# A new order of steps on every engine of a Mamba-2 layer with a ternary feed-forward part

## What is computed

```python
# mixing part, then layer norm
zxbcdt = u @ W_in.T                       # 512 -> 2184: z 1024, x 1024, B 64, C 64, dt 8
dt  = softplus(zxbcdt[..., -8:] + dt_bias)
xBC = silu(causal_conv_4_taps(xBC) + conv_b)
y   = ssd(x, dt, -exp(A_log), B, C) + x * D     # 8 heads of 128, state 64
yg  = y * silu(z)
yn  = yg * rsqrt(mean(yg * yg) + 1e-5) * norm_w
x1  = layernorm(u + yn @ W_out.T)
# feed-forward part, then layer norm
wu, wg, wd = ternary(W_up), ternary(W_gate), ternary(W_down)   # -1, 0, 1 times mean(|W|)
out = layernorm(x1 + (silu(x1 @ wu.T) * (x1 @ wg.T)) @ wd.T)   # 2048 inner features
```

## Time and profile before

| | |
|---|---|
| median of the runs | 1609.8 us |
| the profiled execution, own time | 1608.34 us |
| its span in the trace | 1606.6 us |
| TensorE busy | 1533.0 us, 95% |
| VectorE, ScalarE, GpSimd busy | 59%, 44%, 24% |
| granted TensorE clock, mean | 0.98 |
| HBM traffic | 57 GB/s over the span |

### The profile page before, as it was taken

How to read it: one execution, slowest core, us unless ns; L and a number is a source line. 1 busy time by engine, 2 the same in 40 slices (tenths; PEclk the granted TensorE clock), 3 DMA queues, 4 the chain that set the end, 5 groups by cost and what they waited for, 6 DMA issues and landing times.

```text
span 1606.6 us, 23426 instructions
## 1 busy us (share of the span) xinstructions
PE 1533.0 (95%) x9012; PEld 1300.0 (81%) x9012; DVE 953.7 (59%) x2026; ACT 710.0 (44%) x1364; POOL 391.7 (24%) x504
## 2 busy tenths in 40 slices
...
GB/s 237 66 21 86 86 73 16 85 86 73 39 62 86 86 57 31 86 86 70 18 89 305 71 7 53 1 17 36 7 47 0 53 0 29 25 14 40 0 27 27
DMA packets 38687, 92.38 MB, mean 58 GB/s; under 512 B 4144, under 2 KB 4656, under 8 KB 38576
## 3 DMA queue, kind: packets, MB, share of 16 engines
...
...
## 4 chain that ended last, share of the span: by engine, by line
PE 66%; DVE 18%; ACT 7%; issue 4%; POOL 4%; DMA 1%; SPq 0%; DVEq 0%; POOLq 0%; ACTq 0%
PE ps L366 30%; PE ps L387 14%; PE ps L221 10%; DVE s_mm L771 7%; PE ps L310 6%; DVE s_xact L692 3%; POOL s_mm L997 2%; ACT s_mm L525 2%; PE ps L264 2%; PE ps L281 2%; DVE s_ygr L798 1%; ACT L532 1%; DVE s_bcacc L692 1%; DVE s_sc L731 1%; ACT s_xT L514 1%
## 5 line engine op out<-in xcount | busy, mean ns | idle before, releaser
L366 PE MATMUL ps<-s_x1h,s_tern 128*128 128x512 f32 x1024 | 406.9, 397 | 3.2 <-DVE s_x1l L871 3.2
L366 PE MATMUL ps<-s_x1l,s_tern 128*128 128x512 f32 x1024 | 405.2, 396 | 0.0
L221 PE MATMUL ps<-s_uhi,s_whi 128*128 128x256 f32 x1088 | 323.1, 297 | 20.0 <-DVE s_xact L692 13.8
L221 PE MATMUL ps<-s_ulo,s_whi 128*128 128x256 f32 x1088 | 313.0, 288 | 0.0
L221 PE MATMUL ps<-s_uhi,s_wlo 128*128 128x256 f32 x1088 | 312.5, 287 | 0.0
L881 DVE TENSOR_TENSOR s_hf<-s_sil,ps 128x512 f32<-128x512 f32 x128 | 87.9, 687 | 330.1 <-PE ps L366 330.0
L221 PEld LDWEIGHTS ps<-s_uhi,s_whi 128*128 128x128 f32 x1088 | 211.9, 195 | 56.2 <-DVE s_xact L692 31.1
L366 PEld LDWEIGHTS ps<-s_x1h,s_tern 128*128 128x128 f32 x1024 | 193.3, 189 | 49.5 <-DVE s_tern L865 3.6
L366 PEld LDWEIGHTS ps<-s_x1l,s_tern 128*128 128x128 f32 x1024 | 193.4, 189 | 45.1
L221 PEld LDWEIGHTS ps<-s_ulo,s_whi 128*128 128x128 f32 x1088 | 212.0, 195 | 0.0
L221 PEld LDWEIGHTS ps<-s_uhi,s_wlo 128*128 128x128 f32 x1088 | 211.6, 195 | 0.0
...
## 6 DMA issues: line engine op xcount, KB each, us to landing
...
```

What stands on the lines that cost most here:

```text
L221: o = e.matmul(IPB[r % 3][:, 256 * i:256 * i + 256], wt[:, j, kk, :], u[:, kk, :], start=(m == 0), stop=(m == 11))
L366: o = e.matmul(bank[:], tern[:, j, 512 * mi + 128 * k:512 * mi + 128 * k + 128], x[g % 2][:, k, :], start=(m == 0), stop=(m == 7))
```

## The change

The step functions, their waits and all buffers stay as they are. What changes is the order of the calls: in the written-out first two groups, in the loop body of the slots, and in the written-out change to the feed-forward part, on all five engines. The loops of the feed-forward part stay. No step is added or removed. The diff, with the loop body whole and the rest cut:

```diff
@@ TensorE
-        warm()
-        DT(0); ip(0, 0); dtT(0); ip(0, 1); ip(0, 2); ip(0, 3); CUM(0); ip(0, 4); G(0)
-        ip(0, 5); ip(0, 6); ip(0, 7); ip(0, 8)
-
-        DT(1); dtT(1); TR(0, 0); TR(0, 1); ip(1, 0); ip(1, 1); TR(1, 1); TR(1, 0); CUM(1); ip(1, 2); ip(1, 3)
-        ip(1, 4); Y(0); G(1); ST(0); ip(1, 5); Y(1); OP(0); ip(1, 6); SQ(0); ST(1); ip(1, 7); SQ(1)
-        TR(2, 1); TR(2, 0); ip(1, 8); TR(3, 0); TR(3, 1)
+        warm(); ip(0, 0); DT(0); ip(0, 1); dtT(0); ip(0, 2); ip(0, 3); CUM(0); ip(0, 4); G(0); ip(0, 5); ip(0, 6)
+        DT(1); ip(0, 7); ip(0, 8); dtT(1); TR(0, 0); TR(0, 1); ip(1, 0); ip(1, 1); TR(1, 1); CUM(1); TR(1, 0)
+        ip(1, 2); ip(1, 3); G(1); Y(0); ip(1, 4); ST(0); ip(1, 5); Y(1); OP(0); SQ(0); ip(1, 6); ip(1, 7); ip(1, 8)
+        TR(2, 1); TR(2, 0); ST(1); SQ(1); TR(3, 0); TR(3, 1)
         for n in range(2, NG):
             c = 2 * n - 2
-            DT(n); OP(c - 1); dtT(n); ip(n, 0); ip(n, 1); ip(n, 2); Y(c); CUM(n); ip(n, 3); ip(n, 4); G(n)
-            ST(c); ip(n, 5); OP(c); Y(c + 1); ip(n, 6); SQ(c); ST(c + 1); ip(n, 7); SQ(c + 1)
-            TR(c + 2, 1); TR(c + 2, 0); ip(n, 8); TR(c + 3, 0); TR(c + 3, 1)
+            DT(n); OP(c - 1); dtT(n); ip(n, 0); ip(n, 1); ip(n, 2); Y(c); CUM(n); ip(n, 3); ST(c); G(n); ip(n, 4)
+            ip(n, 5); OP(c); Y(c + 1); SQ(c); ip(n, 6); ip(n, 7); TR(c + 2, 1); TR(c + 2, 0); ip(n, 8); ST(c + 1)
+            TR(c + 3, 0); SQ(c + 1); TR(c + 3, 1)
         c = NCH - 2
-        OP(c - 1); Y(c); ST(c); T1(0, 1); WT(); T1(0, 0); Y(c + 1); SQ(c); T1(0, 2); T1(0, 3); OP(c)
+        OP(c - 1); Y(c); ST(c); WT(); T1(0, 1); T1(0, 0); T1(0, 2); Y(c + 1); SQ(c); T1(0, 3); OP(c); expert(0, 0, 0)
...
@@ ScalarE
         for n in range(2, NG):
             c = 2 * n - 2
-            f_zs(n - 1, 3); f_xTe(c + 1, 1); f_uhi(n); f_E(c); f_E(c + 1); f_xe(n, 0); f_spexp(n); f_dec(c)
-            f_xTe(c + 1, 0); f_dec(c + 1); f_xe(n, 1)
+            f_uhi(n); f_E(c); f_dec(c); f_zs(n - 1, 3); f_xe(n, 0); f_xTe(c + 1, 1); f_dec(c + 1); f_spexp(n)
+            f_xe(n, 1); f_xTe(c + 1, 0); f_xe(n, 2); f_E(c + 1)
             if n == 2:
-                wabs(4); wabs(5)
-            wabs(3 * n); f_silc(n, 0); f_xe(n, 2); f_silc(n, 1); f_sq(c); f_ygh(c); f_xe(n, 3); f_silc(n, 2)
-            wabs(3 * n + 1); f_xe(n, 4); f_seg(c + 2); f_silc(n, 3); f_silc(n, 4); f_sq(c + 1); wabs(3 * n + 2)
-            f_ygh(c + 1); f_zs(n, 0); f_zs(n, 1); f_zs(n, 2)
+                wabs(4)
+            f_silc(n, 0); f_xe(n, 3); f_sq(c)
+            if n == 2:
+                wabs(5)
+            f_ygh(c); wabs(3 * n); f_silc(n, 1); wabs(3 * n + 1); f_xe(n, 4); f_seg(c + 2); f_silc(n, 2); f_silc(n, 3)
+            f_silc(n, 4); wabs(3 * n + 2); f_sq(c + 1); f_zs(n, 0); f_ygh(c + 1); f_zs(n, 1); f_zs(n, 2)
             if n == NG - 1:
-                f_dec(c + 2); f_E(c + 2)
-            f_xTe(c + 2, 0); f_xTe(c + 2, 1); f_seg(c + 3)
+                f_E(c + 2)
+            f_xTe(c + 2, 0); f_xTe(c + 2, 1)
+            if n == NG - 1:
+                f_dec(c + 2)
+            f_seg(c + 3)
...
@@ VectorE
         for n in range(2, NG):
             c = 2 * n - 2
-            f_ms(c - 1); f_dte(n); f_ulo(n); f_M(c); f_dtr(n); f_r1(c - 1); f_dA(n); f_wz(c); f_wz(c + 1)
-            f_taps(n, 0); f_taps(n, 1); f_M(c + 1); f_gate(c, 0); f_gate(c, 1); f_cte(n); f_taps(n, 2); f_sqsum(c)
-            f_GM(n); f_S(c); f_taps(n, 3); f_taps(n, 4); f_dd(c + 2); f_x1(c - 1); f_gate(c + 1, 0); f_gate(c + 1, 1)
+            f_ms(c - 1); f_ulo(n); f_dte(n); f_M(c); f_dtr(n); f_wz(c); f_taps(n, 0); f_dA(n); f_wz(c + 1)
+            f_taps(n, 1); f_gate(c, 0); f_cte(n); f_taps(n, 2); f_S(c); f_gate(c, 1); f_r1(c - 1); f_M(c + 1)
+            f_sqsum(c); f_GM(n); f_taps(n, 3); f_taps(n, 4); f_ms(c); f_gate(c + 1, 0); f_gate(c + 1, 1); f_dd(c + 2)
+            f_r1(c)
             if n < NG - 1:
                 f_dd(c + 3)
-            f_ms(c); f_sqsum(c + 1)
+            f_sqsum(c + 1); f_x1(c - 1); f_x1(c)
             if n == NG - 1:
                 f_M(c + 2); f_wz(c + 2); wtot()
-            f_r1(c); f_S(c + 1); f_x1(c)
+            f_S(c + 1)
...
@@ GpSimd
         for n in range(2, NG):
             c = 2 * n - 2
-            f_Cexp(c); f_DI(c); f_rs(c - 1); f_edge(n, 0); f_xw(c); f_xw(c + 1); f_edge(n, 1); f_rs1(c - 1); f_Sd(c)
-            f_DI(c + 1); f_Cexp(c + 1); f_edge(n, 2); f_ygl(c); f_edge(n, 3); f_edge(n, 4); f_rs(c)
+            f_DI(c); f_Cexp(c); f_edge(n, 0); f_xw(c); f_Sd(c); f_rs(c - 1); f_xw(c + 1); f_edge(n, 1); f_edge(n, 2)
+            f_ygl(c); f_rs1(c - 1); f_Cexp(c + 1); f_DI(c + 1); f_Sd(c + 1); f_edge(n, 3); f_edge(n, 4); f_rs(c)
+            f_rs1(c)
...
@@ SyncE
         for n in range(2, NG):
             c = 2 * n - 2
-            load_bc(c + 2)
+            load_bc(c + 2); load_r0(c); load_wst(3 * n + 1)
             if n < NG - 1:
                 load_u(n + 1)
-            load_wst(3 * n + 1); load_bc(c + 3); load_wst(3 * n + 2); load_r0(c); load_r0(c + 1); load_wst(3 * n + 3)
-            store_x1(c - 1)
+            load_bc(c + 3); load_wst(3 * n + 2); store_x1(c - 1); load_r0(c + 1); store_x1(c)
             if n < NG - 1:
                 store_ct(n + 1)
-            store_x1(c)
-
+            load_wst(3 * n + 3)
...
```

More of the change, by code:

```diff
@@ L429, in program_pe @@
+        expert(0, 11, 1); down(0, 8); T1(1, 3); down(0, 9)
         for g in range(8):
@@ L610, in program_act @@
-        f_seg(0); f_silc(0, 2); f_zs(0, 1); f_silc(0, 3); split_out(4); split_out(6); wabs(1)
-        f_zs(0, 2); f_uhi(1); f_silc(0, 4); f_zs(0, 3); f_spexp(1); f_E(0); f_xTe(0, 0); f_xTe(0, 1); f_xe(1, 0)
-        split_out(3); f_xe(1, 1); f_dec(0); f_xTe(1, 0); f_dec(1); f_seg(1); f_xe(1, 2)
-        split_out(1); split_out(5); f_xTe(1, 1); f_E(1); f_silc(1, 0); f_ygh(0); f_sq(0); wabs(2)
-        split_out(7); f_silc(1, 1); f_xe(1, 3); f_silc(1, 2); f_xe(1, 4); f_seg(2); f_silc(1, 3); f_sq(1)
@@ L616, in program_act @@
-        wabs(3); f_ygh(1); f_zs(1, 0); f_silc(1, 4); f_zs(1, 1); f_zs(1, 2); f_xTe(2, 0); f_xTe(2, 1); f_seg(3)
+        f_uhi(0); split_in(16); split_in(8); expA(); f_xe(0, 0); split_in(9); split_in(10); split_in(12); split_in(11)
+        split_in(13); split_in(14); f_xe(0, 1); split_in(15); f_spexp(0); split_in(1); split_in(0); f_silc(0, 0)
+        split_in(2); split_in(3); f_xe(0, 2); split_in(4); split_in(7); f_xe(0, 3); f_silc(0, 1); f_silc(0, 2)
+        wabs(0); f_xe(0, 4); split_in(6); f_silc(0, 3); split_in(5); split_out(2); f_silc(0, 4); split_out(0)
@@ new lines, in program_act @@
+        f_seg(0); split_out(4); f_zs(0, 0); f_zs(0, 1); f_E(0); f_seg(1); f_uhi(1); split_out(6); f_spexp(1); wabs(1)
+        f_xTe(0, 0); f_zs(0, 2); f_zs(0, 3); split_out(3); f_xTe(0, 1); f_E(1); f_dec(0); f_xe(1, 0); f_xTe(1, 0)
+        split_out(1); f_xe(1, 1); split_out(5); f_xe(1, 2); f_silc(1, 0); f_xTe(1, 1); f_xe(1, 3); f_dec(1)
+        f_silc(1, 1); split_out(7); f_sq(0); f_ygh(0); f_xe(1, 4); wabs(2); f_silc(1, 2); wabs(3); f_seg(2); f_ygh(1)
+        f_sq(1); f_zs(1, 0); f_silc(1, 3); f_zs(1, 1); f_zs(1, 2); f_silc(1, 4); f_seg(3); f_xTe(2, 0); f_xTe(2, 1)
```

88 lines of the change are left out of this document (37 added, 51 removed).

## The result

The kernel after takes **1544.66 us** (median of four runs, 1542.94 to 1546.29) against 1611.32 for the kernel before in the same comparison (1609.1 to 1614.51): a ratio of 0.9585, with a 95% interval of 0.9563 to 0.9606. The forecast was 1546. The profiled execution took 1546.29 us, with a span of 1544.4.

The account below looks back on a forecast made before the run. TensorE, busy 1533.0 of 1606.6 us, bounds the kernel; order wins only pauses and low clock. Gains 42.5 + 4.5 + 3.9 + 3.0 + 10 = 63.9 from 1608.34 give 1544.4, median 1.46 above: 1546 us, range 1530 to 1578.

Parts of the forecast that it names:

- What bounds the kernel: Whole kernel: TensorE busy 1533.0 of 1606.6 us; order can win only its 73.6 us of pauses and low-clock time.
- The slots: Slots 2 to 14: waits and low clock go, a slot comes to 48.9 us, 42.5 us gained.
- The walk: Step times and waits reckoned in the new order, from each slot's start with slot 4's durations; also used for the start.
- the 0.3 a slot: Each slot: waits still booked, 0.1 us for `Y(c + 1)` on `f_DI(c + 1)` and 0.2 for `DT` on `f_ms`.
- The reading of `G`'s wait: Slots: `G` waits, 32.9 us in total, because VectorE's copy of `cum` stands behind `f_M(c + 1)` and two gates.
- Slot 15 and the change: Slot 15 gains 4.5 us; the stretch behind it, to the first expert, gains 3.9 as `OP`'s wait goes.
- The experts: First experts: the 3.2 us wait for `f_x1l` and slow matmuls mostly go; 3.0 us gained, between 0 and 4.8.
- The first two groups: Kernel start, 99.15 us: the walk gives 13 us gained, 10 taken, bounds 0 and 23.
- The stall did not move to `Y(c + 1)`: Rival, slots: the stall moves to `Y(c + 1)`, 1.5 us late each slot, low clock stays: 1577 us, chance 0.20.
- The tables: Rival, slots: two added ScalarE table loads a slot delay `G`: 1561 us, still a gain; slower this way, chance 0.02.
- Start and change bring nothing: Rival, start, change and first experts: weights' DMAs and conversions set them, 10 + 3.9 + 3.0 us given back: 1563, chance 0.12.
- The signs named beforehand: Profile after: right if slots take 48.6 to 49.3 us at clock 1.00; wrong if slots exceed 50 or start 95.

Follow-up runs that it names:

- e9_edge: The kernel before with GpSimd's `f_edge(n, 0)` moved behind the two `f_xw` in the slots, VectorE untouched: 1565.04 us.
- e3_x1l: The kernel before with the slots' new loop bodies, and `f_x1l(1, 0)` and `f_x1l(1, 1)` moved ahead of `ternary(12)` on VectorE: 1549.47 us.
- e6_hold: The kernel after with one wait added on GpSimd: behind `split_in(13)` the splits pause until `f_dA(0)` is done: 1537.27 us.
- e10_splits: `e6_hold` with `split_in(5)` and `split_in(4)` ahead of `f_edge(0, 1)` to `(0, 3)` on GpSimd: 1536.29 us.
- e8_sqsum: The kernel after with `f_sqsum(c)`, 2.1 us of VectorE, put ahead of `f_M(c + 1)` in the slots: 1543.75 us.
- e7_tables: The kernel after with `f_zs(n - 1, 3)` ahead of `f_E(c)` on ScalarE in the slots, so 28 table loads go: 1545.46 us.

## Why the prediction was right, and where it was not

The time, 1544.66 against 1546, is better than its parts, and so close by luck. In the two profiles the start's term was 8.2 us too high, that of the change 2.1 too high, and the other three were too low by 8.6 in sum; the errors cancel to 1.7. What was right and not luck is that the slots give most of it, and why TensorE's pauses go.

- **What bounds the kernel.** Right. All but the last 0.3 us of pauses in slots 2 to 14 went, and with them the low clock: TensorE's busy time there fell from 643.53 to 629.75, where I had reckoned 630.9 for full clock.
- **The slots: 42.5 forecast, 47.3 measured.** The walk's times that mattered hold well: `cum` at 19.0 against 18.9; the last `cd` copy of `f_silc(n, 0)` at 19.6 against 19.7; `f_DI(c + 1)` at 32.3, inside 31.4 to 33.3. Others are further off: `f_DI(c)` is done at 6.5 and not 7.8, `f_dA` at 15.8, past the 15.6 given as its latest, `f_r1(c - 1)` at 24.6 and not 23.4, tap set 4 at 37.0 and not 38.1. None of these used up its margin. Mis-sized was the 0.3 a slot booked for `DT` and `Y(c + 1)`: neither waits. 13 x 0.3 = 3.9, and a slot is 48.53 and not 48.59, another 0.8.
- **The reading of `G`'s wait** was half of it. "Not for work that is late by nature, but for a place in VectorE's queue" named `f_cte`'s place; `e9_edge` shows that the same 33 us go when `f_cte` stays where it is and `f_M` is not held by GpSimd. I had both rows, 4.73 in the earlier trace rows and the pair's 3.80 in the earlier trace rows. I named the hold on `f_M` in a rival, as a danger of the new order, but in the reading of the stall I took 4.73 as the step's length, not as 2.2 of work and 2.5 of hold.
- **Slot 15 and the change: 8.4 forecast, 8.0 measured.** The sum is luck. Slot 15 gained 6.2 and not 4.5: the 1.3 booked for late transposes of the last chunk didn't come, nor did the 0.3. The change gained 1.8 and not 3.9: `OP`'s 4.1 went and the two `Y`s wait 2.0, as booked, but `Y(31)` then waits 1.8 more for `f_S`, which the walk did not have, and the work is 21.3 and not 20.8.
- **The experts: 3.0 forecast, 5.1 measured.** `e3_x1l` shows that the swap gives all of it. I cut the 4.8 of idle time and slow clock to 3.0 for fear of `load_tern`'s DMAs, which were in time: no wait for them stands in TensorE's list.
- **The first two groups: 10 forecast, 1.8 measured, some 4 over all profiles with either start.** This step failed. I had booked the hold in the slots, 2.34 us in place of 0.2 for a small step of `f_dtr`, and I had `skip_diag`'s 5.81 us in the earlier trace rows, four of whose eight instructions took 1.3 us, one per split. I moved it behind `f_dA(0)` and didn't give the same hold to what takes its place. "`f_dtr(0)` and `f_dA(0)` come somewhat later" was 3 us of work become 10. `e6_hold` and `e10_splits` take the hold away and begin slot 2 at 90.08 and 87.41, which is 9.1 and 11.7 us of the 13 that the walk gave. The hold explains 4 to 7 of the missing microseconds; of the rest, 2.5 is `ip(0, 7)`'s wait for `split_in(4)` in `e6_hold`, where the walk had 1.5 for such a wait. `e10_splits` has another order than the one walked, so its 11.7 is no test of the 13. Mistrust of a stretch that shows itself only once made the number smaller, but it did not name the mechanism.
- **The rivals.** The stall did not move to `Y(c + 1)`; `e8_sqsum` loads that chain by 2.1 us more and it still doesn't bind. The tables cost nothing (`e7_tables`). "Start and change bring nothing" was nearer to the truth for both than my sum, 10 + 3.9: they brought 4 or less and 1.8. It was false of the first experts.
- **The signs named beforehand.** `G`'s wait gone, clock 1.00, 30 more table loads, `OP`'s and the expert's waits gone: all seen. Slots came to 48.53, just under the 48.6 to 49.3. Idle time ahead of slot 2 fell from 18.2 to 14.6 us and was not halved; 97.36 is over the 95 that I had named as the sign of a failed start, as is the 95.54 of `e7_tables`; the 94.24 of `e8_sqsum` is just under it.
